# The inverse of a gated delta rule: blocks gathered by ScalarE and transposed on VectorE in place of a trip through DRAM, with split down products, earlier first maxima and a new timetable

## What is computed

```python
# layer 0, attention: a gated delta rule, 16 key heads, 32 value heads (2 to a key head), width 128
qkvz, ba = x @ W_qkvz, x @ W_ba
q, k, v = silu(causal_conv4(mixed(qkvz)))                  # 4 taps along the tokens
q, k = l2norm(q) / sqrt(128), l2norm(k)
M = strictly_lower(beta * k @ k.T * decay)                 # in chunks of tokens
Tinv = inv(eye + M)                                        # unit lower triangular
u, w = Tinv @ (beta * v), Tinv @ (beta * k * exp(g))
for chunk in chunks:                                       # the recurrence over the state S
    v_new = u - w @ S
    o = qg @ S + A @ v_new
    S = S * exp(g_last) + kdecay.T @ v_new
x1 = (rmsnorm(o * silu(z))) @ W_out
# layer 0, feed-forward: ternary weights, hidden 1024
x2 = rmsnorm(silu(x1 @ Wg.T) * (x1 @ Wu.T)) @ Wp.T
# layer 1: attention (16 heads of width 16, 4 KV heads, rope, causal), a mixture of 8 experts (2 to a
# token), and a feed-forward of hidden 1024 with ternary weights
```

## Time and profile before

| | us |
|---|---|
| median of 3 runs | 1549.53 |
| lowest, highest | 1540.88, 1549.71 |
| the profiled execution | 1544.02 |
| its span, first to last instruction | 1542.3 |

### The profile page before, as it was taken

How to read it: one execution, slowest core, us unless ns; L and a number is a source line. 1 busy time by engine, 2 the same in 40 slices (tenths; PEclk the granted TensorE clock), 3 DMA queues, 4 the chain that set the end, 5 groups by cost and what they waited for, 6 DMA issues and landing times. The chain is left out here.

```text
span 1542.3 us, 35670 instructions
## 1 busy us (share of the span) xinstructions
PE 1394.9 (90%) x13996; PEld 1042.2 (68%) x13996; DVE 1046.3 (68%) x2136; ACT 861.7 (56%) x1736; POOL 529.1 (34%) x562
## 2 busy tenths in 40 slices
PE   4459999999999999999999999999899977898998
PEld 3336767677777777677777777767578755555755
DVE  4877685868768686776868778686735536773344
ACT  5555566666666665666666666666355315676210
POOL 1872232332323233232333323333335427441100
PEclk9678999999999999999999999999999988999999
DMA  5112010301111020111102012020211030002000
GB/s 169 37 49 53 16 37 18 67 15 26 33 23 35 19 67 16 26 33 23 36 18 67 23 20 43 13 38 16 57 66 55 33 98 1 1 1 57 27 14 14
DMA packets 142486, 56.39 MB, mean 37 GB/s; under 512 B 109776, under 2 KB 134992, under 8 KB 142064
## 3 DMA queue, kind: packets, MB, share of 16 engines
q1 hardware_dynamic: 133424, 48.20, 13.6%
q10 hardware_dynamic: 8896, 5.91, 1.3%
HBM read 37.11 MB, written 16.97 MB: 35 GB/s over the span
## 5 line engine op out<-in xcount | busy, mean ns | idle before, releaser
L1153 POOL TENSOR_TENSOR og<-og,sz 128x256 f32<-128x256 f32 x128 | 93.2, 728 | 513.5 <-DVE og L1096 295.2
L690 PE MATMUL banks<-wz,xT 128*128 128x256 f32 x512 | 129.0, 396 | 14.1 <-DVE yacc L1116 14.1
L943 DVE SCALAR_TENSOR_TENSOR Yv<-banks,cwall,Yv 128x511 f32<-128x511 f32 (+2 forms) x192 | 130.3, 741 | 6.4 <-ACT Yv L783 6.3
L542 PE MATMUL banks<-wv,xT 128*128 128x512 f32 x256 | 119.0, 608 | 12.5 <-DVE Yv L943 11.0
L542 PE MATMUL banks<-wqk,xT 128*128 128x512 f32 x256 | 122.6, 614 | 0.2 <-DVE Yk L943 0.2
L761 PE MATMUL banks<-wo,oT 128*128 128x256 f32 x512 | 122.6, 382 | 0.0
L690 PEld LDWEIGHTS banks<-wz,xT 128*128 128x128 f32 x512 | 96.1, 195 | 36.9 <-issue 24.2
L930 ACT ACTIVATE junk<-og 128x512 f32<-128x512 f32 x64 | 40.6, 634 | 121.5 <-POOL og L1153 121.5
L1160 POOL TENSOR_TENSOR rn<-ss,c_half 128x4 f32<-128x4 f32 x64 | 64.5, 1007 | 122.0 <-DVE ss L1110 122.0
L761 PEld LDWEIGHTS banks<-wo,oT 128*128 128x128 f32 x512 | 92.6, 190 | 11.5 <-issue 0.7
L734 PE MATMUL banks<-V,A 128*128 128x128 f32 x512 | 85.8, 290 | 9.1 <-ACT V L910 9.1
(11 more groups left out here) (385 smaller groups left out, 3648.8 us busy)
## 6 DMA issues: line engine op xcount, KB each, us to landing
cm_d<-CM SPq DMA_DIRECT2D x32, 256.0 KB, 4.0
wqk<-in_L_attn_W_qkvz SPq DMA_DIRECT2D x8, 512.0 KB, 4.6
wv<-in_L_attn_W_qkvz SPq DMA_DIRECT2D x8, 512.0 KB, 4.2
wz<-in_L_attn_W_qkvz SPq DMA_DIRECT2D x16, 256.0 KB, 2.9
wo<-in_L_attn_W_out SPq DMA_DIRECT2D x16, 256.0 KB, 3.1
blk<-cm_d SPq DMA_DIRECT2D x128, 16.0 KB, 1.8
t_d<-tb SPq DMA_DIRECT2D x16, 128.0 KB, 1.7
Td<-t_d SPq DMA_DIRECT2D x128, 16.0 KB, 1.9
```

The costliest lines, as they stand in the source:

```text
L542: ins = pe.matmul(bank[b][:, :], xT[:, d, b * S + of_batch, :], w[:, d, :], start=(d == 0), stop=(d == KD - 1))
L690: ins = pe.matmul(bank[7][:, b * 256:(b + 1) * 256], xT[:, d, b * S + q, :], wz[:, d, :], start=(d == 0), stop=(d == KD - 1))
L943: v.scalar_tensor_tensor(y, bank[b][:, 0:T - j], conv_w(k, t)[:, 3 - j:4 - j], y, ALU.mult, ALU.add).then_inc(s["tap"].sem, 1)
L1153: pool.tensor_tensor(og[:, n, :, :], og[:, n, :, :], sz[q % 2][:, b, :].rearrange("p (h d) -> p h d", h=VR), ALU.mult).then_inc(s["osz"].s ...
```

## The change

1. **Into the inverse.** ScalarE copies the diagonal 32 x 32 blocks of `CM` in four instructions of 32 partitions x 512 (`act_quarters`) into `t512`, in the order column-major within blocks (reads are 128 elements apart). VectorE transposes all of it at once (128 x 512) into `blk`, and picks with a predicated copy (128 x 256) the half that belongs to the partition. `cm_d`, its 2 + 8 DMAs and the clearing of `blk` go.
2. **Out of the inverse.** VectorE spreads `tb` into `t512` with a product against `own`, which holds one and zero (128 x 512, reads 16 elements apart), and transposes it at once into `Td` (writes 32 elements apart). `t_d`, its 1 + 8 DMAs, and the clearing of `Td` by GpSimd go.
3. **Split down products.** ScalarE copies each hidden tile into float32r (`high`, 16 x 128 x 512), VectorE subtracts (`rest`, 16 x 128 x 512), and PE does 128 float32r products in place of 64 in float32. Those of the first sequence stand ahead of `f0ss`, those of the second behind a wait for `f0ms`.
4. **First maxima ahead.** The 16 maxima of round 0 move from `attention` into `layer1_in`, between its hidden products; keys are turned by sequence, queries earlier. The maxima of round 1 no longer wait for round 0's.
5. **New tables** for stage one, and four pieces of the second ternary weight 4 us apart in place of 6.

```diff
@@ gdn
-    def sp_blocks(sp, k):
-        yield at(k)["cm"]
-        sp.wait_ge(*s["CM"](1, k))
-        for half in halves:
-            sp.dma_start(cm_d[half, :, :], CMf[half, :, half]).then_inc(s["cm_out"].sem, 16)
...
-        yield at(k)["base"]
-        sp.wait_ge(*s["sub"](17, k))
-        sp.dma_start(t_d, tb[:, 0:256].rearrange("p (i c) -> p i c", c=16)).then_inc(s["tu_out"].sem, 16)
...
+    def act_quarters(act, k):
+        yield at(k)["quart"]
+        act.wait_ge(*s["CM"](1, k))
+        if k:
+            act.wait_ge(*s["base"](0, k - 1))
...
+        for g in quarters:
+            ins = act.copy(t512[g, :].rearrange("p (i b m) -> p i b m", b=2, m=16), CMf[g, :, g].rearrange("p m (b i) -> p i b m", b=2))
+        ins.then_inc(s["quart"].sem, 1)
...
     def v_inverse(v, k):
+        yield at(k)["blk"]
+        v.wait_ge(*s["quart"](0, k))
...
+        v.transpose(pairs.rearrange("p i b j -> p (i b j)"), t512[:, :]).then_inc(s["blk"].sem, 1)
+        v.wait_ge(*s["blk"](0, k))
+        v.copy_predicated(pairs[:, :, 0, :], c["odd"][:, :].unsqueeze(2).to_broadcast([P, 16, 16]), pairs[:, :, 1, :]).then_inc(s["blk"].sem, 1)
...
+        yield at(k)["base"]
+        v.tensor_tensor(apart, t16.rearrange("p i c -> p c i").unsqueeze(2).to_broadcast([P, 16, 2, 16]), c["own"][:, :].unsqueeze(1).unsqueeze(3).to_broadcast([P, 16, 2, 16]), ALU.mult).then_inc(s["wide"].sem, 1)
+        v.wait_ge(*s["wide"](0, k))
...
+        v.transpose(Td[:, :, :].rearrange("p m (b c) -> p c b m", b=2), apart.rearrange("p c b i -> p c (b i)")).then_inc(s["base"].sem, 1)
...
-    def pool_inverse(pool, k):
...
-        pool.memset(Td[:, :, :], 0.0).then_inc(s["TU0"].sem, 1)
@@ pe_forward
-        pe.wait_ge(*s["f0h"]())
-        pe.wait_ge(*s["f0acc"]())
...
+        for b in range(B):
+            if b:
+                yield START["f0"] + FSTEP * 17
+                pe.wait_ge(*s["f0acc"]())
...
+                ins.then_inc(s["f0ss"].sem, 1)
+                pe.wait_ge(*s["f0ms"]())
...
+                    for i, part in enumerate((high[8 * b + f], rest(8 * b + f))):
+                        ins = pe.matmul(bank[2 * b + t // 2][:, t % 2 * D:(t % 2 + 1) * D], part[:, t * P:(t + 1) * P], down_r[f // 4][:, f % 4, :], start=(f + i == 0), stop=(f + i == 8))
...
+    def act_down_parts(act):
...
+            act.copy(high[n], hidden(n)).then_inc(s["f0high"].sem, 1)
+
+    def v_down_parts(v):
...
+            v.tensor_tensor(rest(n), hidden(n), high[n].bitcast(F32), ALU.subtract).then_inc(s["f0rest"].sem, 1)
@@ v_second, pe_second, act_second
-            yield START["q1c"] + 6.0 * (g - 6)
+            yield START["q1c"] + 4.0 * (g - 6)
@@ layer1_in
-        for n in range(14):
+        for n in range(7):
             pe_hidden(pe, n)
...
+        pe_keys(pe, 0)
+        for n in (7, 8):
+            pe_hidden(pe, n)
...
+        for i in range(4 * QT):
+            pe_first_max(pe, i)
+            if i == 13:
+                pe_keys(pe, 1)
+            if i % 2 and i < 14:
+                pe_hidden(pe, 9 + i // 2)
@@ attention
-        for i in range(4 * QT):
+        for i in range(4 * QT if r else 0):
```

More of the change, by code:

```diff
@@ L203, in on_vector @@
         ch.step(v.tensor_scalar(t[4][:, :], col[:, :], 4, None, ALU.logical_shift_right))
+        ch.step(v.tensor_copy(c["odd"][:, :], t[3][:, 0:1]))
+        ch.step(v.tensor_copy(c["own"][:, 1:2], t[3][:, 0:1]))
+        ch.step(v.tensor_scalar(c["own"][:, 0:1], c["own"][:, 1:2], -1.0, 1.0, ALU.mult, ALU.add))
         for name in ("lo16",):
@@ L455, in gdn @@
     f0x = [[rounded(f"f0_x_{part}{b}", where, [P, KD, S, P]) for b, where in enumerate(homes)] for part, homes in (("hi", ("GL", "Tf")), ("lo", ("GR", "P4")))]
-    down_f = [line(t).rearrange("p (f d) -> p f d", d=D) for t in (wv, sq)]
+    down_r = [rounded(f"f0_down{i}", where, [P, 4, D]) for i, where in enumerate(("wv", "sq"))]
+    low_r = [rounded(f"f0_low{i}", where, [P, 4, 512]) for i, where in enumerate(("E", "CM", "A0", "vn0"))]
+    high_r = [rounded(f"f0_high_{where}", where, [P, n * 512]) for where, n in (("Yk0", 2), ("P2", 1), ("blk", 1))]
+    high = [line(t)[:, i * 512:(i + 1) * 512] for t, n in ((f0x[0][0], 2), (f0x[1][0], 2), (high_r[0], 2), (high_r[1], 1), (high_r[2], 1), (gate_r, 4), (up_r[0], 2), (up_r[1], 2)) for i in range(n)]
+    rest = lambda n: low_r[n // 4][:, n % 4, :]
     hid = [line(t) for t in (E, CM, A[0], vn[0])]
@@ L858, in act_inverse @@
         else:
-            act.wait_ge(*s["zero"](4))
+            act.wait_ge(*s["zero"](2))
         for g in range(2):
@@ L1397, in act_forward @@
             if n == 0:
-                act.wait_ge(*s["sub"](17, LAST))
+                act.wait_ge(*s["base"](0, LAST))
             elif n == 8:
@@ L1631, in on_scalar @@
                     act_hidden(act, 2 * (i - 1) + n)
-        for n in range(10, 14):
+        for n in range(10, 15):
             act_hidden(act, n)
-        for g in (0, 1):
-            act.wait_ge(*s["kTt"](g))
-            act.copy(kT[:, g, :, :], bank[g].bitcast(BF16).rearrange("p (t i) -> p t i", t=TT)).then_inc(s["kTa"].sem, 1)
-        for n in range(14, 16):
-            act_hidden(act, n)
+        for u in range(2):
+            act.wait_ge(*s["kTt"](2 + u))
+            act.copy(kT[:, 2 * u:2 * u + 2, QT:TT, :], bank[2 + u].bitcast(BF16).rearrange("p (g t i) -> p g t i", g=2, t=QT)).then_inc(s["kTa"].sem, 1)
+        act_hidden(act, 15)
     def act_turned_x(act, t):
@@ L1679, in on_tensor @@
         pe_qkv(pe, QT - 1)
-        for n in range(14):
+        for n in range(7):
             pe_hidden(pe, n)
-        pe.wait_ge(*s["ks"]())
-        pe.wait_ge(*s["xTe"]())
-        pe.wait_ge(*s["vp"]())
-        for g in range(KVH):
-            for t in range(TT):
-                ins = pe.transpose(bank[g].bitcast(BF16)[:, t * P:(t + 1) * P], ks[:, t, g, :], c["identb"][:, :])
-            ins.then_inc(s["kTt"].sem, 1)
+        pe_keys(pe, 0)
+        for n in (7, 8):
+            pe_hidden(pe, n)
         pe.wait_ge(*s["slots"](4))
@@ L1694, in on_tensor, with pe_keys, pe_first_max @@
             ins.then_inc(s["qTt"].sem, 1)
-        for n in range(14, 16):
-            pe_hidden(pe, n)
+        pe.wait_ge(*s["xTe"]())
+        pe.wait_ge(*s["masks"]())
+        pe.wait_ge(*s["kTe"]())
+        for i in range(4 * QT):
+            pe_first_max(pe, i)
[3 more added lines that the diff above has]
+                pe_hidden(pe, 9 + i // 2)
+    def pe_keys(pe, b):
+        pe.wait_ge(*s["ks"](2 * b + 1))
+        if b == 0:
+            pe.wait_ge(*s["vp"]())
+        for u in range(2):
+            if b:
+                pe.wait_ge(*s["kTe"](u))
+            for g in range(2):
+                for t in range(QT):
+                    ins = pe.transpose(bank[2 + u].bitcast(BF16)[:, (g * QT + t) * P:(g * QT + t + 1) * P], ks[:, b * QT + t, 2 * u + g, :], c["identb"][:, :])
+            ins.then_inc(s["kTt"].sem, 1)
+    def pe_first_max(pe, i):
+        t, g = divmod(i, KVH)
+        width = (t + 1) * P
+        if t == 0:
+            pe.wait_ge(*s["qTe"](g // 2))
+        if i >= 2:
+            pe.wait_ge(*s["mx"](i - 2))
+        pe.matmul(bank[i % 2][:, 0:width], qT[0:USED, g, t, :], kT[0:USED, g, 0:t + 1, :], start=True, stop=False, skip_group_check=True)
+        pe.matmul(bank[i % 2][:, width - P:width], c["identb"][:, :], by_query[:, :], start=False, stop=True, skip_group_check=True).then_inc(s["sc"].sem, 1)
     def on_gpsimd(pool):
@@ L1737, in on_gpsimd @@
             ins.then_inc(s["ks"].sem, 1)
-        pool.memset(qs[:, :, :, USED:P], 0.0).then_inc(s["slots"].sem, 1)
-        for b in range(B):
-            for i, part in enumerate(Q_PARTS):
-                ins = pool.tensor_copy(qs[:, b * QT:(b + 1) * QT, :, i * HD:(i + 1) * HD], seats(b, part))
-            ins.then_inc(s["slot"].sem, 1)
+            if j % 2:
+                for i, part in enumerate(Q_PARTS):
+                    ins = pool.tensor_copy(qs[:, 2 * j - 2:2 * j + 2, :, i * HD:(i + 1) * HD], seats(j // 2, part))
+                ins.then_inc(s["slot"].sem, 1)
     on_sync(nc.sync)
@@ L1933, in rounds @@
     def rounds(engine, *kinds):
-        in_order([(ROUND * r, f(engine, r)) for r in range(N) for f in kinds if r or f not in (pe_first, act_first)])
+        in_order([(ROUND * r, f(engine, r)) for r in range(N) for f in kinds if r or f not in (pe_first, act_first, pe_max)])
     def on_gpsimd(pool):
```

161 lines of the change are left out of this document (84 added, 77 removed), and 83 rows, old and new, of tables (AT, ATTN, FINAL, FIRST).

## The result

The changed kernel takes 1575.69 us (median of 4 runs, 1572.07 to 1579.14) against 1549.62 of before in the same comparison: ratio 1.0176, 95% interval 1.0148 to 1.0204. It is slower by 26 us. The forecast was 1521, the range ended at 1540. The profiled execution has a span of 1573.5 us where before had 1542.3.

What follows compares the result with a forecast made beforehand. Stage one was taken as bound by PE's own work. From the profiled 1544.0 us, less 10.5 (turns), 12 (down products) and 3 (first maxima), 1518.5; plus 2.5 towards the median, 1521 us; range 1502 to 1540.

Steps and rivals of the forecast that it cites:

- The copies, x = 0.68 us: Four ScalarE copies ahead of V[0] in each turn: 0.68 us each, making PE wait 0.4 us a turn at AV[0].
- My own formula: PE's wait for V at AV[0] is 4x - 2.3 us a turn, x being the time of one ScalarE copy.
- Rival (d): Slower through ScalarE's gather: decides at x = 1.1 us a copy; at x = 1.5, 1570 us; chance 0.06.
- The base inverse begins at about the time it did: In stage one's turns: the base inverse starts about when it did, so VectorE's added work costs nothing on the path.
- P16's wait for Td, -0.54 us a turn: In stage one, PE's wait for the DMA bringing Td back goes, since two VectorE instructions replace 27 DMA steps: 0.54 us a turn.
- y[3] ahead of sub3, -0.6 us: In stage one's turns, zp's 0.68 us wait for y goes when y[3] precedes sub3: about 0.6 us a turn.
- VectorE at nothing: VectorE's added 2.9 to 3.3 us a turn in stage one costs nothing, covered by 16.6 us idle a turn.
- Turn 0: Stage one's first turn, set by VectorE: 3 us more ahead of the value's taps, no inverse wait; 0, -3 to +3.
- Down products: End of stage one: split float32r products in place of float32 save 12 us, bounds 8 to 15.
- rival (b): VectorE sets stage one's end: differences and ternary pieces queue ahead of f0ms and y; down products gain 6 us; 1527; chance 0.11.
- First maxima, -3: layer1_in and attention: round 0's maxima taken ahead gain 3 us, bounds 0 and 6.
- rival (a): Stage one stays as it is: copies cost 0.87 us or more, PE waits 1.2 us a turn; 1531.5; chance 0.25.

Runs made afterwards that it cites:

- e2: Changed kernel, the four ScalarE copies taking the same elements in another order: reading runs of 32 neighbours, writing 128 bytes apart; 1575.24 us, ratio 1.0167.
- e6: Changed kernel with 60 instructions ahead on PE's queue, two of the four copies moved behind z and VectorE's transpose moved later; 1561.02 us, ratio 1.0103.
- e10: Changed kernel with 60 instructions ahead on PE's queue and the first two double products of pw moved ahead of AV[0]; 1555.27 us, ratio 1.0046.
- e7: Kernel before with 60 instructions (waits) ahead on PE's queue; 1534.81 us, ratio 0.9927.
- e3: Changed kernel with 60 more instructions (waits) at the start of PE's queue; 1554.84 us, ratio 1.005.
- e5: Changed kernel with copies reading neighbours (gathering left out, inverse of other numbers) and 60 instructions ahead on PE's queue; 1526.88 us, ratio 0.9878.
- e11: Kernel before with the split down products and 60 instructions ahead on PE's queue; 1527.85 us, ratio 0.9855.
- e4: Changed kernel with the first maxima taken back into attention, layer1_in as before; 1575.66 us, ratio 1.0177.
- e12: Kernel before with split down products, first maxima ahead and 60 instructions ahead on PE's queue; 1525.19 us, ratio 0.9846.
- e8: Kernel before with the split down products alone; 1539.62 us, ratio 0.997.
- e1: Changed kernel, the four ScalarE copies reading 512 neighbouring elements of CM (gathering left out, inverse of other numbers); 1545.75 us, ratio 0.9987.

## Why the prediction was wrong, step by step

Three steps failed: the price of ScalarE's copies, the gain put down for the DMA and for y, and the ends of the instruction blocks, which had no term. The forecast has the fifteen turns 11.1 us shorter (0.74 a turn before rounding) and they came out 34.1 longer. Of these 45.2 us, 22.0 are the copies (28.0 where 6 were put), 15.7 the gains (1.4 where 17.1 were put) and 7.5 the block ends.

**The copies, x = 0.68 us: wrong, and the largest term.** Measured 1.07. My upper bound, 0.87, carried the loss of L1028 over per instruction (0.37 us) to another engine; no row stood behind that ceiling, and a spread ScalarE access loses 0.46. My own formula was right: 4 x 1.07 - 2.3 = 2.0 us of wait, 1.7 measured. Rival (d) was the mechanism; its threshold, x = 1.1, was met to within 3%, and it had 0.06 because I took half of one bound for the value. But its formula gives 1545 us at x = 1.07, level with before; the other 31 us lie in the terms below, so it had the mechanism and not the size. The rule cited against the change (the Trainium skill, SBUF — State Buffer, section Door 1: each access that crosses into another line of 16 bytes pays) pointed the right way, and e2 says that it holds for a spread writing side too.

**What queues behind the new wait: left out.** I named V[0], V2[0] and z[0] behind the copies on ScalarE, but not what stands behind VectorE's wait for them. "The base inverse begins at about the time it did" holds, and says nothing of S[0], og[0] and `AT`, which in the old order did not stand behind `blk`. e6 and e10 show it: with PE's wait for V gone, 15 to 19 us of wait for `AT` stand there. The inverse's first instruction (`sub0`) does stand where it stood, 15.15 us ahead of P16 in most turns (14.5 to 15.9 us in turns 2 to 14 of before).

**P16's wait for Td, -0.54 us a turn: gone, and nothing gained.** No wait for Td is left, as forecast, but the ends of blocks stop PE for 12.0 us at the same line, and e7 loses the wait with the trip still in place. The hint stood in the same group, the 1.1 us "issue" at the same line: it is a block's end (turn 6, after 103 products), and I added it to the DMA's account instead of asking why a wait would have no releaser.

**Block ends: not in the sum at all.** 19.6 us of the changed kernel's time (e3's U0 against after's), 12.1 of before's; the difference, 7.5 us, is part of the loss.

**y[3] ahead of sub3, -0.6 us: right as to the wait, not as to the gain.** No wait for y is left; V's 7.7 and most of the silu's 5.3 us went too. But R (5.3 to 7.0 us) and oT (2.6 to 4.0) came instead, so in e5 the new order nets 0.1 us a turn. "VectorE at nothing" was wrong by R's 0.5 to 0.6 us a turn, which PE's wait at L704 shows, as I had named for that case.

**Turn 0: 4.6 us longer**, 0 +- 3 forecast. 3.1 of them are in PE's first wait for VectorE (18.1 against 21.2 us). Not tried.

**Down products: right.** -10.5 us in the changed kernel, -12.4 in e11, -12 forecast. The wait between f0ss and the second sequence was 2.5 us (1.7 forecast), for f0ms as forecast; rival (b) is out. (The working has 27.6 us for products that took 29.4 by its own times; the first eight, at 3.35 us, are not in its spacing of 1.73.)

**First maxima, -3: wrong by its size.** The stage grew by 6.0 us for 6.6 forecast, attention gave back 3.1 where 9.6 were needed. e4 and e12 put the part at 0 to 3 us.

**The chances** have a slip: 0.78 for a time under 1534 counts 0.09 of rival (a)'s 0.25, which is not "a good half".

Put together, from the table (the terms close by construction): before's 1012.1 us of fifteen turns, less its own block ends (12.1), less the new order's gain (1.4), plus the spread copies (28.0), plus the block ends of after (19.6) are the 1046.2 measured.

## What to carry to other kernels

Ask of a new instruction in a full schedule not only what it delays on its own queue but which other engine waits for it, and what stands behind that wait; serving one of two customers moves nothing. A price that no row shows has no upper bound from another engine's row: keep the slow side of it in the range when four of them stand ahead of the critical path sixteen times. When a wait has no releaser and its position shifts by a constant from turn to turn, count instructions; and when a wait is for a DMA, look whether an instruction packet lies beside it. A few idle instructions at the head of the queue are a cheap test of both, and here worth 11 us in the kernel before.

## What the runs showed of the hardware

PE's instructions arrive in pieces of 16.4 KB, 256 instructions. An end of one in a run of 128 short products (118 in 1.20 us) stopped PE for 0.3 to 2.1 us where it fell behind the 95th (e8) to the 120th (e1). It did so where the packet started at most 1.1 us ahead of the run's first product, and PE went on 2.3 to 2.7 us behind the packet's start; where the packet had started 1.3 us ahead or sooner, there was no pause. In before and e8, whose blocks end at the same places, the packets start at different times and the pauses differ with them. What sets their start was not found.

A chain of eight small DMAs took 6.0 to 6.6 us in seven turns in which an instruction packet started among them, and 5.0 to 5.3 us in fifteen turns in which none did (two of before, thirteen of e7); in turn 14 of before they took 5.8 us without one.

ScalarE's copy of 512 elements a partition takes 0.61 us with neighbours on both sides and 1.07 with one side spread, no matter which, at distances of 128 and 512 bytes.
